# Last mixture of experts: second weights stationary in two parts, the activation evaluated twice, a feature-major output, gates spread by DMA, and one pipeline over all blocks

## The chip, the cores and the metric

The program runs on one core of a Trainium2 chip. The metric is device microseconds (us) of that core. The kernel before takes 2481.97 us, the median of 3 runs (2480.72 to 2484.28).

Engines are named as the profile names them: PE is TensorE's matmul and PEld its weight load, DVE is VectorE, ACT is ScalarE, POOL is GpSimd, SP is SyncE, which here only issues DMAs.

## What is computed

Four layers follow each other on x, of 4096 tokens by 128 features, each as `x = x + layernorm(layer(layernorm(x)))`. Only the last is touched: a mixture of 8 experts, each with a hidden width of 512, all of them evaluated for every token. Cut from the reference:

```python
logits = x @ router_W + router_b
w, idx = jax.lax.top_k(logits, K)            # K = 2
w = jax.nn.softmax(w, axis=-1)
gates = jnp.einsum('bske,bsk->bse', jax.nn.one_hot(idx, E), w)
xhat = (x - mu) * jax.lax.rsqrt(var + EPS)
h = xhat[:, :, None, :] * ln_g + ln_b
a = jax.nn.gelu(jnp.einsum('bseh,ehf->bsef', h, W1) + b1, approximate=False)
y = jnp.einsum('bsef,efh->bseh', a, W2) + b2
y = y + x[:, :, None, :]
out = jnp.einsum('bseh,bse->bsh', y, gates)
```

## The kernel before

Names of this layer's buffers begin with md_ in the profile. The 4096 tokens are 8 blocks (`NBLK`) of 512 tokens (`BLK`), a block is 4 tiles of 128 tokens (`BPT`), and the hidden width is 4 chunks of 128 (`FC`). One block of one expert is called an item here; there are 64.

**Setting up.** Row statistics of X, transposed and normalised tokens in two parts (`nh`, the rounded value, and `nl`, the rest), W1 in two parts (`wh`, `wl`), router logits, and the router, which leaves `gate` (token-major, 128 x 32 x 8) and `gsum`. W2 is loaded into `w2` as it is.

**The blocks.** PE, DVE, ACT and POOL each run a loop over the 8 blocks.

- PE, per item: 4 calls of `up`, each three matmuls of 512 columns (`matmul_split`, lines 64 to 66) into one bank of `ub`, in turn with 4 calls of `down`, each for one tile of 128 tokens: 4 matmuls at line 2332 with a slice of `a` stationary and W2 moving, in plain float32. The profile counts each such matmul as two records. `down` of an item begins when all four chunks are through ACT.
- ACT, per item: 4 Gelus of 128 x 512 from `ub` to `a` (line 2179).
- DVE, per block: the normalised tokens (2261), times `gsum` (2265), 32 additions of a bias times a gate (2270), then per item 4 additions of an output tile times its gate (2276), then the layer norm of the result (`FinishNorm.vector`, 1476 to 1489) with one power on POOL (1516) in its middle.
- SP stores each block when DVE is done with it (2154).

The output is token-major here: a gate is one number per partition, `gate[:, tile, e]`, and it enters DVE's instruction as that. At a block's end PE waits for all of its Gelus and additions:

```python
pe.wait_ge(gelu, (n + 1) * NE * FC)
pe.wait_ge(acc_done, n * NA + NA)
```

Of the kernel before, what the change touches and what calls it, by code (L numbers as in the profile page):

```python
# [2080 lines left out]
FC = FF // P  # L2081


def ffn_layer1(nc, dr, X, g, out):

    with Mem(nc, "d_") as m:
        wh = m.sb("wh", [P, NE, FF], F32R)
        wl = m.sb("wl", [P, NE, FF], F32R)
        w2 = m.sb("w2", [P, NE, FC, D])
        b1 = m.sb("b1", [P, NE, FC])  # L2090
        b2 = m.sb("b2", [P, NE, D])
# [23 lines left out]
        ub, db = bk[:, 0:FC, :], bk[:, FC:FC + 2, :]
        bp = bk[:, 2 * GRP - 1, :]

        w_in = m.sem("w_in")
# [14 lines left out]
        l_done = m.sem("l_done")  # L2133
        summed = m.sem("summed")
        ln = m.sem("ln")
        up_mm = m.sem("up_mm")
        gelu = m.sem("gelu")
        down_mm = m.sem("down_mm")
        acc_done = m.sem("acc_done")
        stored = m.sem("stored")  # L2140
        NA = BPT * (1 + 2 * NE)
        group = range(GRP)
        firsts = range(0, NBLK, GRP)
        with nc.Block() as block:
            @block.sync
            def _(sp):
                for dst, src in ((raw[:, :, :], "d_w1"), (lng[:, :], "d_lng"), (lnb[:, :], "d_lnb"),
                                 (rr[:, :], "d_wr"), (b1raw[:, :, :], "d_b1")):
                    sp.dma_start(dst, dr[src]).then_inc(w_in, 16)
                for dst, src in ((w2[:, :, :, :], "d_w2"), (b2[:, :, :], "d_b2"), (rbias[:, :], "d_rbias")):  # L2150
                    sp.dma_start(dst, dr[src]).then_inc(c_in, 16)
                with sp.Fori(0, NBLK) as n:
                    sp.wait_ge(F.step, n * F.N + F.N)
                    sp.dma_start(out.rearrange("(t p) d -> p t d", p=P)[:, bass.ds(n * BPT, BPT), :],
                                 X[:, bass.ds(n * BPT, BPT), :]).then_inc(stored, 16)
                sp.wait_ge(stored, 16 * NBLK)

            @block.scalar
            def _(act):
                act.wait_ge(w_in, 16 * 5)  # L2160
                nc.scalar.activation(wr[0][:, :], rr[:, :], ACT.Copy).then_inc(hi, 1)
                for e in range(NE):
                    nc.scalar.activation(wh[:, e, :], raw[:, e, :], ACT.Copy, scale=lng[:, e:e + 1]).then_inc(hi, 1)
                for n in firsts:
                    for i in group:
                        act.wait_ge(xt_mm, n + i + 1)
                        nc.scalar.activation(nh[:, (n + i) * BLK:(n + i + 1) * BLK], bk[:, 2 * i, :],
                                             ACT.Copy).then_inc(xh_done, 1)
                    for i in group:
                        act.wait_ge(l_mm, n + i + 1)  # L2170
                        nc.scalar.activation(lt[:, i, :], bk[0:32, 2 * i + 1, :], ACT.Copy).then_inc(l_copied, 1)
                router.scalar(nc, act)
                with act.Fori(0, NBLK) as n:
                    for e in range(NE):
                        for c in range(FC):
                            act.wait_ge(up_mm, (n * NE + e) * FC + c + 1)
                            if e >= 2 and c == 0:
                                act.wait_ge(down_mm, n * NE + e - 1)
                            nc.scalar.activation(a[:, e % 2, c, :], ub[:, c, :], ACT.Gelu,  # L2179
                                                 bias=b1[:, e, c:c + 1]).then_inc(gelu, 1)  # L2180

            @block.gpsimd
            def _(pool):
                stats_pool(nc, pool, S)
                with pool.Fori(0, NBLK) as n:  # L2185
                    F.pool(nc, pool, n, S)

            @block.vector
            def _(dve):
# [58 lines left out]
                dve.wait_ge(c_in, 16 * 3)  # L2248
                logits(0)
                low(GRP)  # L2250
                weights(range(NE // 2, NE))
# [5 lines left out]
                with dve.Fori(0, NBLK) as n:  # L2257
                    tiles = [bass.ds(n * BPT + s, 1) for s in range(BPT)]

                    for s in range(BPT):  # L2260
                        nc.vector.tensor_scalar(xi[:, s, :], X[:, tiles[s], :], S.mean[:, tiles[s], 0], S.r[:, tiles[s]],
                                                ALU.subtract, ALU.mult).then_inc(ln, 1)
                    for s in range(BPT):
                        dve.wait_ge(ln, n * BPT + s + 1)
                        nc.vector.tensor_scalar(acc[:, s, :], xi[:, s, :], gsum[:, tiles[s]], None,
                                                ALU.mult).then_inc(acc_done, 1)
                    for e in range(NE):
                        for s in range(BPT):
                            dve.wait_ge(acc_done, n * NA + e * BPT + s + 1)
                            nc.vector.scalar_tensor_tensor(acc[:, s, :], b2[:, e, :], gate[:, tiles[s], e], acc[:, s, :],  # L2270
                                                           ALU.mult, ALU.add).then_inc(acc_done, 1)
                    for e in range(NE):
                        dve.wait_ge(down_mm, n * NE + e + 1)
                        for s in range(BPT):
                            dve.wait_ge(acc_done, n * NA + (NE + e) * BPT + s + 1)
                            nc.vector.scalar_tensor_tensor(acc[:, s, :], db[:, e % 2, s * P:(s + 1) * P],  # L2276
                                                           gate[:, tiles[s], e], acc[:, s, :], ALU.mult,
                                                           ALU.add).then_inc(acc_done, 1)
                    dve.wait_ge(acc_done, n * NA + NA)
                    F.vector(nc, dve, n, acc, X, S)  # L2280

            @block.tensor
            def _(pe):
# [32 lines left out]
                pe.wait_ge(c_in, 16 * 3)  # L2316
                with pe.Fori(0, NBLK) as n:
                    cols = bass.ds(n * BLK, BLK)

                    def up(e, c):  # L2320
                        if e > 0:
                            pe.wait_ge(gelu, (n * NE + e - 1) * FC + c + 1)
                        cs = slice(c * P, (c + 1) * P)
                        matmul_split(nc, ub[:, c, :], wh[:, e, cs], wl[:, e, cs], nh[:, cols], nl[:, cols]).then_inc(up_mm, 1)

                    def down(e, s):
                        if s == 0:
                            pe.wait_ge(gelu, (n * NE + e + 1) * FC)
                            if e >= 2:
                                pe.wait_ge(acc_done, n * NA + (NE + e) * BPT)  # L2330
                        for c in range(FC):
                            last = nc.tensor.matmul(db[:, e % 2, s * P:(s + 1) * P], a[:, e % 2, c, s * P:(s + 1) * P],  # L2332
                                                    w2[:, e, c, :], start=(c == 0), stop=(c == FC - 1))
                        if s == BPT - 1:
                            last.then_inc(down_mm, 1)

                    for c in range(FC):
                        up(0, c)
                    for e in range(NE):
                        for s in range(BPT):  # L2340
                            if e + 1 < NE:
                                up(e + 1, s)
                            down(e, s)
# [16 lines left out]
def host_layout(a):  # L2360
# [54 lines left out]
    z["d_b2"] = np.broadcast_to(a["L1_ffn_b2"], (P, NE, D))  # L2415
# [27 lines left out]
```

## Time and profile before

| | us |
|---|---|
| median of 3 runs | 2481.97 |
| profiled execution, its own time | 2475.36 |
| its span, first to last instruction | 2473.6 |
| of it: last mixture, from its first load to the end | 1983.4 to 2473.6 |
| of it: first to last matmul of the blocks | 2026.3 to 2463.9 |

| engine | busy over the span | busy from 2030 to 2474 |
|---|---|---|
| PE | 2078.5 us (84%) | 417.55 us (94%) |
| DVE | 1605.4 us (65%) | 187.81 us (42%) |
| ACT | 999.2 us (40%) | 184.90 us (42%) |
| POOL | 655.3 us (26%) | 8.05 us (2%) |

Times in the rows are counted from the span's start. A row of the timeline is: start, duration, engine, line, operation, output <- input, count, and in brackets the idle time before it with what ended it. Neighbours of one kind are merged into a row with a count, so that duration over count is the pace at which they follow each other; the mean of one (in the groups by line) is longer than that, since neighbours overlap. PEclk is the granted clock of PE as a share of full speed.

### The profile page before, as it was taken

To read this page: it belongs to the slowest core of one execution; us is meant where nothing else is said; L and a number is where in the kernel's file an instruction comes from. 1 tells how busy PE (TensorE), PEld (TensorE's weight loads), DVE (VectorE), ACT (ScalarE), POOL (GpSimd) and SP (SyncE) were. 2 spreads that over 40 slices of the span, in tenths; PEclk is the share of its full clock that TensorE was granted. 3 is DMA by queue.
4 is the path that set the end of the run, shared out by engine and by line. 5 is a ranking of instruction groups with operands and counts; after the bars stand their busy time and mean duration, and the time that the engine had idled before them with its cause. 6 is when DMAs were issued, how large, how long until landed. Compare 5 with 4: busy or idle time off the path is not lost. (4 is left out here: it accounts for less than half of the span.)

```text
span 2473.6 us, 46736 instructions
## 1 busy us (share of the span) xinstructions
PE 2078.5 (84%) x16920; PEld 1650.4 (67%) x16920; DVE 1605.4 (65%) x4182; ACT 999.2 (40%) x1990; POOL 655.3 (26%) x409
## 2 busy tenths in 40 slices
PE   4888888884799988999768885889689869999998
PEld 3667767664456655666556774678477758888887
DVE  5776676774777737777377678677767775333344
ACT  2455455453155552555432222233223334444443
POOL 3545545543145551555400003000300010000000
PEclk9999999997599996999889998899899969999999
DMA  4111111111000000000000001000000020000000
GB/s 154 70 69 58 61 63 65 65 69 36 0 1 2 1 1 1 1 2 1 1 1 0 0 0 41 1 1 1 1 1 1 1 79 5 4 4 4 4 4 8
DMA packets 34795, 54.88 MB, mean 22 GB/s; under 512 B 7104, under 2 KB 16960, under 8 KB 33856
## 3 DMA queue, kind: packets, MB, share of 16 engines
q1 hardware_dynamic: 34624, 52.57, 5.8%
q8 instruction: 111, 1.82, 0.3%
q14 instruction: 60, 0.49, 0.1%
HBM read 16.90 MB, written 2.10 MB: 8 GB/s over the span
## 5 line engine op out<-in xcount | busy, mean ns | idle before, releaser
L1051 POOL TENSOR_TENSOR mb_psum<-mb_pt 128x1024 f32<-128x1024 f32 x112 | 267.1, 2387 | 313.5 <-ACT mb_pt L1031 312.8
L1031 ACT ACTIVATE mb_pt<-mb_stb 128x1024 f32<-128x1024 f32 x256 | 249.2, 1021 | 146.7 <-PE mb_stb L1132 146.2
L2332 PEld LDWEIGHTS md_bk<-md_w,md_a 128*128 128x128 f32 x2048 | 264.0, 192 | 26.2 <-ACT md_a L2179 3.9
L2179 ACT ACTIVATE md_a<-md_bk,md_b 128x512 f32<-128x512 f32 x256 | 175.5, 687 | 244.9 <-PE md_bk L66 244.5
L919 DVE TENSOR_REDUCE mb_mxp<-mb_p1b 128x1 f32<-128x512 f32 x352 | 231.1, 683 | 65.9 <-PE mb_p1b L1116 62.0
L2332 PE MATMUL md_bk<-md_w,md_a 128*128 128x128 f32 x2048 | 267.9, 276 | 2.7 <-DVE md_acc L2276 2.1
L2276 DVE SCALAR_TENSOR_TENSOR md_acc<-md_bk,md_gate,md_acc 128x128 f32<-128x128 f32 x256 | 71.9, 344 | 235.9 <-PE md_bk L2332 235.8
L351 DVE TENSOR_TENSOR ma_tr<-ma_pbank,ma_cs 128x512 f32<-128x512 f32 x256 | 161.6, 682 | 73.3 <-PE ma_pbank L66 69.2
L1955 ACT ACTIVATE mc_p<-mc_sb,mc_nb 128x512 f32<-128x512 f32 (+3 forms) x160 | 98.0, 621 | 186.9 <-DVE mc_nb L1843 186.9
L495 ACT ACTIVATE ma_e<-ma_sbank,ma_mx 128x80 f32<-128x80 f32 x512 | 120.3, 385 | 117.5 <-DVE ma_mx L358 117.5
L2033 PE MATMUL mc_pv<-mc_v,mc_pt 128*128 128x128 f32 x1088 | 149.8, 282 | 11.7 <-DVE mc_pt L1892 11.4
L1116 PE MATMUL mb_p1b<-mb_ks,mb_qs 96*128 96x512 f32 x352 | 152.6, 479 | 6.1 <-DVE mb_qs L912 2.8
L2033 PEld LDWEIGHTS mc_pv<-mc_v,mc_pt 128*128 128x128 f32 x1088 | 134.0, 192 | 23.0 <-DVE mc_pt L1892 18.7
L444 POOL TENSOR_TENSOR ma_qt<-ma_tr,ma_swp 128x512 f32<-128x512 f32 x64 | 88.1, 1378 | 224.3 <-DMA ma_swp<-ma_tr 217.8
L1132 PE MATMUL mb_stb<-mb_qs,mb_ks 98*128 98x512 f32 x512 | 144.7, 404 | 0.8 <-ACT mb_pt L1031 0.8
L1143 PE MATMUL mb_pvb<-mb_pt,mb_v 128*32 128x256 f32 x2048 | 137.0, 385 | 0.0
L64 PE MATMUL md_bk<-md_nh,md_wh 128*128 x256 | 122.9, 480 | 15.2 <-DVE md_acc L2276 12.5
L1516 POOL TENSOR_TENSOR md_frs<-md_fve,md_half 128x4 f32<-128x4 f32 x8 | 8.1, 1007 | 461.8 <-DVE md_fve L1481 461.8
L919 DVE TENSOR_REDUCE mb_mxp<-mb_misc 128x1 f32<-128x512 f32 x160 | 109.1, 682 | 22.0 <-PE mb_misc L1116 22.0
L64 PE MATMUL ma_pbank<-ma_xth,ma_wh 128*128 128x256 f32 x256 | 87.1, 340 | 38.5 <-DVE ma_tr L351 38.4
L1132 PEld LDWEIGHTS mb_stb<-mb_qs,mb_ks 98*128 98x128 f32 x512 | 94.6, 190 | 33.4 <-issue 12.4
L1833 DVE TENSOR_REDUCE mc_mp<-mc_sb 128x1 f32<-128x512 f32 (+3 forms) x160 | 96.6, 609 | 26.1 <-PE mc_sb L2012 13.8
(329 smaller groups left out, 4838.3 us busy)
## 6 DMA issues: line engine op xcount, KB each, us to landing
ma_swp<-ma_tr SPq DMA_DIRECT2D x256, 128.0 KB, 2.0
mg_X<-x SPq DMA_DIRECT2D x4, 512.0 KB, 10.4
ma_cs<-cs SPq DMA_DIRECT2D x1, 2048.0 KB, 9.4
mc_cs<-cs SPq DMA_DIRECT2D x1, 2048.0 KB, 8.1
md_raw<-d_w SPq DMA_DIRECT2D x1, 2048.0 KB, 7.3
md_w<-d_w SPq DMA_DIRECT2D x1, 2048.0 KB, 10.9
out<-mg_X SPq DMA_DIRECT2D x8, 256.0 KB, 2.3
ma_raw<-w_qkv SPq DMA_DIRECT2D x1, 1536.0 KB, 8.4
```

The lines of the kernel that those rows point to most:

```text
L64: nc.tensor.matmul(out, lhs_hi, rhs_hi, start=start, stop=False)
L351: nc.vector.tensor_tensor(tr[:, G % TRS, part, :, :], pbank[:, i % 2, :].rearrange("p (c t) -> p c t", c=2), cs[:, b // 2, part, None, :]. ...
L495: nc.scalar.activation(e[:, s, slot, :], sbank[:, 2 * j + k // 4, k % 4 * KEYS0:(k % 4 + 1) * KEYS0], ACT.Exp, bias=mx[:, s, slot:slot + 1 ...
L919: nc.vector.tensor_reduce(mxp[:, r // NCH, r % NCH:r % NCH + 1], pass_bank(r), AXX, ALU.max).then_inc(p1_max, 1)
L1031: nc.scalar.activation(pt[:, T % RING, :, :].rearrange("p (b h) q -> p b (h q)", b=2), stb[:, 2 * (i % 2):2 * (i % 2) + 2, :], ACT.Exp, sc ...
L1051: nc.gpsimd.tensor_tensor(psum[:, n % SUMS, :, :], pt[:, T % RING, :, :], pt[:, (T + 1) % RING, :, :], ALU.add).then_inc(summed, 1)
L1116: nc.tensor.matmul(pass_bank(r), qs[V % 3][0:QROWS, h, t * P:(t + 1) * P], ks[0:QROWS, c * BLK:(c + 1) * BLK], start=True, stop=True).then ...
L1132: last = nc.tensor.matmul(stb[:, 2 * (i % 2) + hp, :], ks[:, i * P:(i + 1) * P], qs[U % 3][:, 2 * hp:2 * hp + 2, :].rearrange("p h q -> p ...
L1143: last = nc.tensor.matmul(pvb[h * DK:(h + 1) * DK, 0:UQ], v1[:, i, :], pt[:, T % RING, h, :], start=(i == 0), stop=(i == KT - 1), skip_gro ...
L2033: last = nc.tensor.matmul(pv[:, 0:D], pt[:, k % 2, a * P:(a + 1) * P], v[:, c * BPT + a, :], start=(c == 0 and a == 0), stop=(c == chunks[ ...
L2179: nc.scalar.activation(a[:, e % 2, c, :], ub[:, c, :], ACT.Gelu, bias=b1[:, e, c:c + 1]).then_inc(gelu, 1)
L2332: last = nc.tensor.matmul(db[:, e % 2, s * P:(s + 1) * P], a[:, e % 2, c, s * P:(s + 1) * P], w2[:, e, c, :], start=(c == 0), stop=(c == F ...
```

## The change

- **W2 in two parts.** `w2` is replaced by `w2h`, the rounded value (8 copies on ACT, 2216), and `w2l`, the rest (8 subtractions on POOL). The load goes into `late`, whose room later holds the spread gates `gb` (4 rows of 128 x 512), the accumulators `accT` (2) and `tmp` (2).
- **Feature-major output.** `down` works by chunks: three matmuls of 512 columns with a chunk of W2 stationary and the hidden values moving, accumulated over the 4 chunks into a bank of `db` that holds 128 features by 512 tokens.
- **The hidden values in two parts.** ACT evaluates each chunk twice, in full to `a` (2230) and rounded to `ah` (2236), for chunks 0 to 2; chunk 3's rounded value is a copy on DVE. DVE subtracts: `al = a - ah`, 4 per item.
- **Gates.** They now run along the free axis and must be the same on all partitions. Per block PE transposes `gate` to 8 x 512 (2456), ACT copies it to `gT` on partitions 0 to 7 (2223), and SP spreads one row per item over 128 partitions: 64 DMAs of 256 KB whose source is a single partition (2193). DVE then does one `(db + b2) * gb` per item, and POOL adds it to the accumulator.
- **Back to tokens.** Per block PE transposes the accumulator back (2489), and DVE finishes the block in 13 parts (`finish`), two places per item, during later items. The power on POOL and the stores on SP are placed among other items' work too.
- **No loops, no waits at a block's end.** Each engine's 64 items are written out. The DMA for item j is issued when item j-4 has been scaled, and DVE waits for item j's row before it scales item j.

```diff
 @block.sync
-with sp.Fori(0, NBLK) as n:
-    sp.wait_ge(F.step, n * F.N + F.N)
-    sp.dma_start(out..., X[:, bass.ds(n * BPT, BPT), :]).then_inc(stored, 16)
+for j in range(ITEMS):
+    n, e = divmod(j, NE)
+    if e == 0:
+        sp.wait_ge(gT_done, n + 1)
+    if j >= GB:
+        sp.wait_ge(scaled, j - GB + 1)
+    sp.dma_start(gb[:, j % GB, :], gT[e:e + 1, n % 2, None, :].to_broadcast([1, P, BLK])).then_inc(gb_in[j % GB], 16)
+    if e == STORE_AT[1] and n >= STORE_AT[0]:
+        store(n - STORE_AT[0])
 @block.scalar
-nc.scalar.activation(a[:, e % 2, c, :], ub[:, c, :], ACT.Gelu, bias=b1[:, e, c:c + 1]).then_inc(gelu, 1)
+turn_gates(0)
+for j in range(ITEMS):
+    for c in range(FC):
+        hidden(j, c)
+        if c < HIA:
+            high(j, c)
+    if e == GATE_AT and n + 1 < NBLK:
+        turn_gates(n + 1)
 @block.gpsimd
+for e in range(NE):
+    pool.wait_ge(w2_hi, e + 1)
+    nc.gpsimd.tensor_tensor(w2l[:, e, :, :], w2raw[:, e, :, :], w2h[:, e, :, :].bitcast(F32), ALU.subtract)
+for j in range(ITEMS):
+    if e > 0:
+        pool.wait_ge(scaled, j + 1)
+        nc.gpsimd.tensor_tensor(accT[:, n % 2, :], accT[:, n % 2, :], tmp[:, e % 2, :], ALU.add).then_inc(added, 1)
 @block.vector
+def scale(j):
+    dve.wait_ge(down_mm, (j + 1) * FC)
+    dve.wait_ge(gb_in[j % GB], 16 * (j // GB + 1))
+    nc.vector.scalar_tensor_tensor(dst, db[:, j % 2, :], b2[:, e:e + 1], gb[:, j % GB, :], ALU.add, ALU.mult)
+for j in range(ITEMS):
+    low(j, 0)
+    low(j, 1)
+    finish_at(2 * j)
+    high(j, 3)
+    low(j, 2)
+    if j > 0:
+        scale(j - 1)
+    low(j, 3)
+    finish_at(2 * j + 1)
 @block.tensor
-def down(e, s):
-    for c in range(FC):
-        last = nc.tensor.matmul(db[:, e % 2, s * P:(s + 1) * P], a[:, e % 2, c, s * P:(s + 1) * P],
-                                w2[:, e, c, :], start=(c == 0), stop=(c == FC - 1))
-pe.wait_ge(gelu, (n + 1) * NE * FC)
-pe.wait_ge(acc_done, n * NA + NA)
+def down(j, c):
+    if j >= 2:
+        pe.wait_ge(scaled, j - 1)
+    pe.wait_ge(lo_done, j * FC + c + 1)
+    matmul_split(nc, db[:, j % 2, :], w2h[:, e, c, :], w2l[:, e, c, :], ah[:, c, :], al[:, c, :],
+                 start=(c == 0), stop=(c == FC - 1)).then_inc(down_mm, 1)
```

On PE, one piece of an item. In the kernel before, in the loop over the blocks:

```order
L64 MATMUL md_bk<-md_nh,md_wh 128x512
L65 MATMUL md_bk<-md_nh,md_wl 128x512
L66 MATMUL md_bk<-md_nl,md_wh 128x512
L2328 ISA
L2330 REGISTER_ALU
L2332 MATMUL md_bk<-md_w,md_a 128x128 x4
```

The same place in the changed kernel, at the item in which the accumulator of the block before is turned back (`md_late`):

```order
L64 MATMUL md_bk<-md_nh,md_wh 128x512
L65 MATMUL md_bk<-md_nh,md_wl 128x512
L66 MATMUL md_bk<-md_nl,md_wh 128x512
L2489 MATMUL md_bk<-mg_ident,md_late 128x128 x4
L64 MATMUL md_bk<-md_ah,md_w2h 128x512
L65 MATMUL md_bk<-md_ah,md_w2l 128x512
L66 MATMUL md_bk<-md_al,md_w2h 128x512
```

Three float32r matmuls of 512 columns stand where four float32 matmuls of 128 columns stood; the transposes come once per block.

On SP, the queue of the stores, `+` and `-` as the change makes them:

```order
-L2154 DMA out<-mg_X 128x4x128
-L2152 REGISTER_ALU
-L2152 COMPARE_AND_BRANCH
-L2144 UNCONDITIONAL_BRANCH
...
+L2179 DMA md_late<-d_w 128x4096
+L2193 DMA md_late<-md_raw 128x1x512 x23
+L2184 DMA out<-mg_X 128x4x128
+L2193 DMA md_late<-md_raw 128x1x512 x8
+L2184 DMA out<-mg_X 128x4x128
```

A loop with nothing but stores became a queue in which 23 spreads of a gate row (`md_late<-md_raw` is `gb` from `gT`) stand ahead of the first store and 8 ahead of each later one, until the last two blocks.

On ACT, the end of setting up and the first item:

```order
+L2216 ACTIVATE md_w2h<-md_late 128x512 x8
 L1544 ACTIVATE md_r_ex<-md_r_df 128x32
```

The 8 roundings of W2 now stand ahead of the router's exponential.

## Rows read from the trace of the kernel before

**Rows 1.** Busy time and clock over the blocks (engines, PEclk, DMA share, GB/s).

```profile
2030.00:2474.00 444.00, 417.55 (x2804) 377.41 (x2804) 187.81 (x769) 184.90 (x264) 8.05 (x8) 0.97 0.02 5
```

**Rows 2.** Groups by line, 2030 to 2474: count, busy us, mean ns, idle before.

```profile
L2332 PE MATMUL md_bk<-md_w,md_a 128*128 128x128 f32 x2048 | 267.9, 276 | 2.7 <-DVE md_acc L2276 2.1 <-ACT md_a L2179 0.4
...
L2179 ACT ACTIVATE md_a<-md_bk,md_b 128x512 f32<-128x512 f32 x256 | 175.5, 687 | 244.9 <-PE md_bk L66 244.5
...
L2276 DVE SCALAR_TENSOR_TENSOR md_acc<-md_bk,md_gate,md_acc 128x128 f32<-128x128 f32 x256 | 71.9, 344 | 235.9 <-PE md_bk L2332 235.8
```

**Rows 3.** Timeline, PE inside a block: one `up` and one `down`.

```profile
2201.71 0.48 PE L64 MATMUL md_bk<-md_nh,md_wh 128*128 x1
...
2202.26 0.39 PE L66 MATMUL md_bk<-md_nl,md_wh 128*128 x1
...
2202.49 1.05 PE L2332 MATMUL md_bk<-md_w,md_a 128*128 128x128 f32 x8
...
2203.29 0.48 PE L64 MATMUL md_bk<-md_nh,md_wh 128*128 x1
```

**Rows 4.** Timeline, PE from one block into the next.

```profile
2197.38 0.63 PE L65 MATMUL md_bk<-md_nh,md_wl 128*128 x1
...
2197.81 0.63 PE L66 MATMUL md_bk<-md_nl,md_wh 128*128 x1
```

**Rows 5.** Timeline of neighbours on ACT and DVE; one DVE line.

```profile
2030.45 3.00 ACT L2179 ACTIVATE md_a<-md_bk,md_b 128x512 f32<-128x512 f32 x5
...
2020.37 2.48 DVE L2204 TENSOR_TENSOR md_nl<-md_bk,md_nh 128x512 fp32r<-128x512 f32 x4 [0.62 <-ACT md_nh L2167]
...
2022.77 2.73 DVE L2225 SCALAR_TENSOR_TENSOR md_wl<-md_raw,md_lng,md_wh 128x512 fp32r<-128x512 f32 x4
...
L1632 DVE TENSOR_SCALAR mb_rq<-mb_rq,mb_g x1: 415/415/415, 613.0 to 613.0; 128x384 f32<-128x384 f32 x1
```

**Rows 6.** Timeline, DVE finishing one tile by rows, in the layer before.

```profile
1979.50 0.35 DVE L1508 TENSOR_SCALAR mc_acc<-mc_acc,mc_fmv,mc_frs 128x128 f32<-128x128 f32 x1 [1.12 <-POOL mc_frs L1516]
...
1980.20 0.34 DVE L1508 TENSOR_SCALAR mc_acc<-mc_acc,mc_fmv,mc_frs 128x128 f32<-128x128 f32 x1
```

**Rows 7.** Timeline, POOL and DVE on two SBUF inputs together, and POOL alone.

```profile
1526.37 1.30 POOL L1913 TENSOR_TENSOR mc_rp<-mc_tr 128x512 f32<-128x512 f32 x1 [0.68 <-DVE mc_tr L1803]
...
1526.39 1.83 DVE L1809 TENSOR_TENSOR mc_kql<-mc_rp,mc_kqh 128x512 fp32r<-128x512 f32 x1
...
L446 POOL TENSOR_TENSOR ma_kt<-ma_tr,ma_swp x64: 1262/1275/2331, 48.2 to 556.3; 128x512 f32<-128x512 f32 x64
```

**Rows 8.** DMA: issues (KB each, us to landing), and a stretch of loads.

```profile
ma_swp<-ma_tr SPq DMA_DIRECT2D x256, 128.0 KB, 2.0
...
out<-mg_X SPq DMA_DIRECT2D x8, 256.0 KB, 2.3
...
1988.00:1996.00 8.00, 1.61 (x7) 1.17 (x7) 7.79 (x54) 3.62 (x7) 8.00 (x4) 0.50 1.00 410
```

**Rows 9.** Timeline, start of the blocks on PE, ACT and DVE.

```profile
2019.05 1.97 PE L2291 MATMUL md_bk<-mg_ident,md_xn 128*128 128x128 f32 x16
...
2026.31 0.49 PE L64 MATMUL md_bk<-md_nh,md_wh 128*128 x1 [0.89 <-DVE md_lg L2212]
...
2022.18 2.69 ACT L2171 ACTIVATE md_lt<-md_bk 32x512 f32<-32x512 f32 x4 [0.38 <-PE md_bk L66]
...
2029.15 1.28 ACT L2179 ACT_TABLE_LOAD   x1
...
2036.24 0.42 DVE L2255 TENSOR_REDUCE md_gsum<-md_gate 128x32 f32<-128x256 f32 x1
```

**Rows 10.** Timeline, tail: DVE, POOL and SP after the last item.

```profile
2459.01 4.85 PE L2332 MATMUL md_bk<-md_w,md_a 128*128 128x128 f32 x40
...
2466.71 1.01 POOL L1516 TENSOR_TENSOR md_frs<-md_fve,md_half 128x4 f32<-128x4 f32 x1 [52.59 <-DVE md_fve L1481]
...
2469.89 0.38 SPq L2154 DMA_DIRECT2D out<-mg_X  x1
```

More of the change, by code:

```diff
@@ L2081 @@
 FC = FF // P
+GB = 4
+GATE_AT = 3
+STORE_AT = (2, 6)
+POWER_AT = (1, 4)
+APPLY = (10, 12)
+FINISH_AT = 2 * (NE + 2)
 def ffn_layer1(nc, dr, X, g, out):
@@ L2105, in ffn_layer1 @@
         gsum = m.sb("gsum", [P, TILES])
+        ah = m.sb("ah", [P, FC, BLK], F32R)
+        al = m.sb("al", [P, FC, BLK], F32R)
         xn = m.sb("xn", [P, GRP, BPT, D])
@@ L2135, in ffn_layer1 @@
         ln = m.sem("ln")
+        w2_in = m.sem("w2_in")
+        w2_hi = m.sem("w2_hi")
+        w2_lo = m.sem("w2_lo")
         up_mm = m.sem("up_mm")
         gelu = m.sem("gelu")
+        hi_act = m.sem("hi_act")
+        hi_dve = m.sem("hi_dve")
+        lo_done = m.sem("lo_done")
         down_mm = m.sem("down_mm")
-        acc_done = m.sem("acc_done")
+        scaled = m.sem("scaled")
+        added = m.sem("added")
+        gT_mm = m.sem("gT_mm")
+        gT_done = m.sem("gT_done")
+        gb_in = [m.sem(f"gb_in{k}") for k in range(GB)]
+        turned = m.sem("turned")
+        row_sum = m.sem("row_sum")
         stored = m.sem("stored")
-        NA = BPT * (1 + 2 * NE)
+        ITEMS = NBLK * NE
+        HIA = FC - 1
         group = range(GRP)
@@ L2247, in _ @@
                 dve.wait_ge(inv_step, 2)
-                dve.wait_ge(c_in, 16 * 3)
+                dve.wait_ge(c_in, 16 * 2)
                 logits(0)
@@ L2256, in _ @@
                 dve.wait_ge(summed, 1)
[L2257 to L2280, printed above, removed]
@@ new lines, in finish @@
+                def finish(n, part):
+                    s = part // 2
+                    if part < 2 * BPT:
+                        if part % 2 == 0:
+                            residual(n, s)
+                            total(n, s)
+                        else:
+                            dve.wait_ge(row_sum, n * BPT + s + 1)
+                            F.row_stats(nc, dve, n, s, acc)
+                    elif part in APPLY:
+                        for k in range(2):
+                            s = 2 * APPLY.index(part) + k
+                            F.apply(nc, dve, n, s, acc, X, n * BPT + s)
@@ new lines, in _, with finish_at @@
+                PARTS = APPLY[-1] + 1
+                def finish_at(t):
+                    n, part = divmod(t - FINISH_AT, 2 * NE)
+                    if 0 <= n < NBLK and part < PARTS:
+                        finish(n, part)
+                for j in range(ITEMS):
[8 more added lines that the diff above has]
+                    finish_at(2 * j + 1)
@@ L2282, in _ @@
+                scale(ITEMS - 1)
+                for t in range(2 * ITEMS, FINISH_AT + 2 * NE * (NBLK - 1) + PARTS):
+                    finish_at(t)
             @block.tensor
@@ new lines, in _, with turn_gates, up @@
+                pe.wait_ge(c_in, 16 * 2)
+                def turn_gates(n):
+                    pe.wait_ge(summed, 1)
+                    if n > 0:
+                        pe.wait_ge(gT_done, n)
+                    for s in range(BPT):
+                        last = nc.tensor.transpose(gtb[:, s * P:(s + 1) * P], gate[:, n * BPT + s, :], ident[:, :])
+                    last.then_inc(gT_mm, 1)
+                def up(j, c):
+                    n, e = divmod(j, NE)
+                    cols = slice(n * BLK, (n + 1) * BLK)
+                    cs = slice(c * P, (c + 1) * P)
+                    if j >= 1:
+                        pe.wait_ge(gelu, (j - 1) * FC + c + 1)
+                        if c < HIA:
+                            pe.wait_ge(hi_act, (j - 1) * HIA + c + 1)
+                    matmul_split(nc, ub[:, c, :], wh[:, e, cs], wl[:, e, cs], nh[:, cols], nl[:, cols]).then_inc(up_mm, 1)
@@ new lines, in turn_back @@
+                def turn_back(n):
+                    pe.wait_ge(added, (n + 1) * (NE - 1))
+                    if n > 0:
+                        pe.wait_ge(row_sum, n * BPT)
+                    for s in range(BPT):
+                        last = nc.tensor.transpose(fb[:, s * P:(s + 1) * P], accT[:, n % 2, s * P:(s + 1) * P], ident[:, :])
+                    last.then_inc(turned, 1)
+                for c in range(FC):
+                    up(0, c)
+                turn_gates(0)
+                for j in range(ITEMS):
+                    n, e = divmod(j, NE)
+                    for c in range(FC):
+                        if j + 1 < ITEMS:
+                            up(j + 1, c)
+                        if c == 2 and e == GATE_AT and n + 1 < NBLK:
+                            turn_gates(n + 1)
+                        if c == 2 and e == 1 and n > 0:
+                            turn_back(n - 1)
+                        down(j, c)
@@ L2348, in rope_tables @@
+                turn_back(NBLK - 1)
 def rope_tables(n, d, scale):
```

132 lines of the change are left out of this document (92 added, 40 removed).

## Prediction

> **What bounds the kernel now.** I read the busy times first: over the blocks of the last mixture PE is busy 417.55 of 444 us, at 0.97 of full clock, while DVE and ACT have less than 190 us of work each and the DMA engines almost none [rows 1]. Then the groups by line: ACT's Gelus sat idle 244.5 us for PE and DVE's additions 235.8 us, whereas the matmuls of `down` waited 2.7 us in all [rows 2]. So PE sets the pace, and in the timeline one reads off what it is made of. Inside a block an `up` and a `down` follow each other every 2203.29 - 2201.71 = 1.58 us [rows 3], four times per item: 6.32 us, and 64 items are 404.5 us. The matmuls run from 2026.31 to 2463.86 [rows 9, 10], which is 437.5 us. The other 33 us lie at the start and at the block ends, where PE stands still and then runs at half clock: a matmul of 512 columns follows the last after 0.43 us there [rows 4] and after 0.23 us inside a block [rows 3].
>
> **What the change takes from PE.** `up` stays: three matmuls at 0.23, 0.695 us. `down` of one tile took 1.58 - 0.695 = 0.885 us; it becomes the same triple as `up`, 0.695 us. An item then costs PE 8 x 0.695 = 5.56 us in place of 6.32, and 64 cost 356 us. Transposes are added, 8 per block at 1.97/16 = 0.12 us [rows 9], with their breaks some 8 us in all. The stops at the block ends go, if nothing else is late.
>
> **ACT.** Seven evaluations per item instead of four. Their mean is 0.687 us [rows 2] but neighbours follow at 3.00/5 = 0.60 [rows 5], so 4.2 us per item, 4.8 if each took its full mean. Both are under 5.56. One copy of gates per block adds 0.6 us. The table load of 1.28 us, once per block before, now comes once.
>
> **DVE.** Per item: four subtractions at 2.48/4 = 0.62 (the form of the row is the same but reads one input from PSUM), one rounding copy, at 128 x 512 scaled from 0.415 us for 384 columns to about 0.5, one scaling by the spread gates at 2.73/4 = 0.68 [rows 5]. That is 3.7 us. The finish of a block costs per tile four short instructions of at most 0.345 us [rows 2] with a break of 0.1 between dependents, 1.6 us, and 0.70 us for the last two [rows 6]; four tiles 9.2 us, 1.15 per item. Sum 4.8 us, under 5.56.
>
> **POOL.** One addition of 128 x 512 in 7 of 8 items, 1.27 us alone [rows 7], hidden by far. But it does not leave DVE alone. In the layer before, a DVE subtraction of two SBUF inputs that began 0.02 us behind a POOL addition took 1.83 us and ended 0.55 us behind the other's end [rows 7]; alone such a one takes about 0.68. So DVE stood still for the whole of POOL's 1.27. At worst this adds 1.1 us to an item: 4.8 + 1.1 = 5.9 us. The addition comes right behind DVE's scaling, with one subtraction in front of it and the finish parts behind, so I take less than half.
> The Trainium skill has this as a rule ("SBUF — State Buffer", section "Who interferes with whom": a DVE instruction with two SBUF inputs contends with a GpSimd instruction that reads SBUF, and the second fully blocks). The row agrees with it.
>
> **The gates' DMAs.** Per item SP spreads one row of 2 KB, on one partition, over 128: 256 KB. They are issued four items ahead, about 16 us before they are needed at 5.56 per item, so latency is no question; what matters is how often one can be served. No row shows a source on a single partition, so I bound it.
> - From below: 128 KB from 64 partitions to 64 others lands after 2.0 us and 256 KB from 128 partitions to memory after 2.3 [rows 8]. At that price the DMAs are hidden with 3 us to spare per item.
> - From above: in the busiest 8 us of loads 16 DMA engines moved 410 GB/s at a busy share of 1.00 [rows 8], 25.6 GB/s each. Each then had 8 partitions of its own. If the limit is the way into those partitions rather than the engine, sixteen engines reading one partition share one such way: 262144 B / 25.6 GB/s = 10.2 us per item, almost twice what PE needs.
> The loads came from memory, which may have slowed them a little; I take 9.5 us for a copy inside SBUF, and keep 10.2. Between 2.3 and 9.5 I take the upper end, with some doubt: the steady, even share of the sixteen in the loads looks like sixteen separate ways, and none of these rows has more than one engine at one partition.
> The Trainium skill puts it as a rule ("SBUF — State Buffer", section "Door 1: The DMA port swizzle": partitions map to 16 ports, and a transfer reaches only the ports of its partitions, 27.2 GB/s each). One partition is one port, and by its figure a row would take 9.6 us, 64 of them 617 us; by the landing times above it would cost nothing. Nothing in this trace tests it for a read.
>
> **Setting up and the tail.** The router's end stays at 2036.66 [rows 9]. The 8 roundings of W2 (0.6 each) stand between ACT's last copy at 2024.87 and the router's exponential, done by 2029.9, while DVE still looks for indices until 2033.3; POOL's 8 subtractions end 8 x 1.27 behind 2025.6, at 2035.8. So neither is late. But ACT now waits for the gates before its first Gelu: transposes 0.5, copy 0.6, breaks 0.2, first spread issued at 2038.0, table load, first Gelu at 2039.4, where it was 2030.45 [rows 5]. That costs about 9 us of start. Tail, behind the last matmul or the last gate row: scaling 0.85, addition 1.4, transposes 0.7, four tiles at 1.6, power 1.4, four at 0.7, store and landing 2.7, in all 16 us; before it was 9.7 (2463.86 to the end).
>
> **The sum.** If one partition limits the DMAs: 2038.0 + 64 x 9.5 + 1.7 (fixed part of a landing) = 2647.7, tail 16, span 2663.5. The profiled execution took 1.8 more than its span and the median lies 6.6 above that: 2663.5 + 8.4 = **2672 us**. At 10.2 it is 2717. That PE idles 4 us per item then and may lose clock is covered: even at 0.43 us per matmul in part of an item it has 9.5.
>
> **Rivals.**
> 1. *The DMAs are hidden and PE bounds* (faster, the other side). From 2040.8: 63 x 2.78 + 64 x 2.78 = 353, transposes 8, filling and small stalls 10, PE ends at 2412; tail 16, span 2428: **2436 us** (2425 to 2450). For it speak the landing times of 2.0 and 2.3; against it, that none has a single source partition. It decides at a price per DMA of about 5.7 us: below, this is the result.
> 2. *The DMAs are hidden, and DVE and POOL take turns.* 6.0 us per item with breaks, 64 x 6.0 = 384, from 2040.8 and with the tail: 2441, or **2450 to 2465 us** with the transposes' stalls. For it speaks the 1.83; against it, that DVE has unshared work (scaling, statistics) to lay beside the addition.
> 3. *The row is served at half of an engine's rate*, since one partition is an eighth of what an engine served: 19 us per item, past 3200 us. I see no row for it.
>
> **How the numbers follow.** One-partition limit at 9 to 10.2 us per row: 0.56. Rival 1: 0.31. Rival 2: 0.09. Rival 3 or another slow case: 0.02. A DMA price between 6 and 7 that ends near the old time: 0.02. The forecast's own range is 2640 to 2720. Over all cases 8 in 10 need both sides: 2426 to 2720. About 0.2% is what a measurement of this kernel can tell from no change. Faster 0.40, same 0.01, slower 0.59.
>
> **What would show it.** Right: the spread DMAs land 25 to 40 us behind their issue (four are queued), the DMA queue moves about 27 GB/s through the whole stage, DVE's scaling waits for the DMA, PE is busy about 60% of an item, and POOL, ACT and DVE idle. Rival 1: landing near 2.5 us, PE over 95% busy at full clock, an item every 5.6 us. Rival 2: DVE over 95% with subtractions of 1.2 us and more in each item. The PE step is wrong if a triple of `down` is not 0.70 us; ACT's is if its pace is nearer 0.69 than 0.60. The forecast falls as a whole if one partition can feed more than 46 GB/s (256 KB in 5.7 us).

## The result, and the profile after

The changed kernel takes 2639.16 us (median of 4 runs, 2636.08 to 2640.48); the kernel before took 2483.12 beside it. The ratio is 1.063 (95% interval 1.061 to 1.065): slower by 156 us, all of it in the last mixture. The layers ahead are the same code, but they end up to 11 us earlier or later from one execution to the next. So this text measures the *stage*: from the MEMSET of line 714, with which DVE enters the last mixture, to the end of the span. Each stage is that of one profiled execution; differences of 1 or 2 us between stages are not read. Before it was 2473.6 - 1983.49 = 490.1 us, after it is 2636.5 - 1991.20 = 645.3.

The page of the kernel after, part 1, and of part 2 the granted clock, the DMA engines' busy tenths and what they moved, in 40 slices of 66 us. The last nine slices are the blocks of the last mixture:

```profile
PE 2098.4 (80%) x15704; PEld 1600.2 (61%) x15704; DVE 1751.6 (66%) x4054; ACT 1120.0 (42%) x2191; POOL 758.8 (29%) x473
...
PEclk8999999996899969998799879998996798888887
DMA  4111111110000000000000100000001788888886
GB/s 144 67 63 65 65 65 59 67 38 33 1 1 1 1 1 1 1 1 1 0 0 0 38 1 1 1 2 1 1 1 66 25 32 32 34 34 32 34 34 35
```

The DMA engines, all but idle before at this place (share 0.02, 5 GB/s in [rows 1]), are now 80 to 90% busy in seven of the last nine slices and yet move only 32 to 34 GB/s there. A stretch of loads moved 410 at share 1.00 [rows 8]. Then 50 us inside the blocks as a window (columns as in [rows 1]), and below it two short stretches, which are used further down:

```profile
2150.00:2200.00 50.00, 40.25 (x148) 29.70 (x149) 31.29 (x61) 27.62 (x43) 12.01 (x8) 0.90 0.88 33
...
2145.00:2155.00 10.00, 7.65 (x26) 5.52 (x26) 5.04 (x10) 3.40 (x5) 1.67 (x1) 0.84 0.90 27
2155.50:2158.50 3.00, 2.94 (x15) 1.96 (x13) 0.00 (x0) 1.42 (x3) 0.00 (x0) 1.00 0.85 49
```

PE is busy 80% of the 50 us, at a granted clock of 0.90 in the mean, where it was 94% busy at 0.97 over the blocks before. No engine is full. The issues of DMAs (KB each, median us to landing):

```profile
md_late<-md_raw SPq DMA_DIRECT2D x64, 256.0 KB, 29.9
...
out<-mg_X SPq DMA_DIRECT2D x8, 256.0 KB, 19.7
```

The spread rows land 29.9 us behind their issue. The stores, same size and same queue, needed 2.3 us before [rows 8] and now 19.7: they wait their turn behind the spreads. Who waits, over 2040 to 2637 (total us, times, longest):

```profile
DVE md_late L2364 <- issue: 196.3, 43, 6.6
...
PE md_bk L64 <- DVE md_al L2344: 126.2, 50, 3.9
ACT md_raw L2230 <- DVE md_al L2344: 105.7, 44, 3.8
...
DVE md_late L2364 <- DMA md_late<-md_raw: 25.7, 5, 5.5
```

Line 2364 is the scaling by the spread gates. DVE stands in front of it 43 times, and the view gives "issue", which means that it saw nothing that released it. Only in 5 cases does it name the DMA. In 8 more (22.3 us) it names PE's L66, and the matmuls of PE show that this is not what held DVE (one of the 8):

```profile
2150.96 0.40 PE L66 MATMUL md_bk<-md_al,md_w2h 128*128 128x512 f32 x1
...
2157.35 0.39 PE L66 MATMUL md_bk<-md_al,md_w2h 128*128 128x512 f32 x1
...
2158.74 0.75 DVE L2364 SCALAR_TENSOR_TENSOR md_late<-md_bk,md_b,md_late 128x512 f32<-128x512 f32 x1 [4.59 <-PE md_bk L66]
```

The scaling at 2158.74 needs the four chunks of its item. The last of them is the first row, done at 2151.36; the second row belongs already to the next item. In all 8 the item's last matmul began 4.4 us or more ahead of its scaling. What holds DVE there is read from the rhythm, in the timeline of DVE, and of SP's DMA issues at the same time (the second fence):

```profile
2300.86 0.75 DVE L2364 SCALAR_TENSOR_TENSOR md_late<-md_bk,md_b,md_late 128x512 f32<-128x512 f32 x1 [2.23 <-PE md_bk L66]
...
2310.88 0.75 DVE L2364 SCALAR_TENSOR_TENSOR md_late<-md_bk,md_b,md_late 128x512 f32<-128x512 f32 x1 [4.80 <-issue]
...
2320.68 0.75 DVE L2364 SCALAR_TENSOR_TENSOR md_late<-md_bk,md_b,md_late 128x512 f32<-128x512 f32 x1 [5.15 <-issue]
2321.34 2.37 DVE L2344 TENSOR_TENSOR md_al<-md_raw,md_ah 128x512 fp32r<-128x512 f32 x2
```

```profile
2289.43 17.45 SPq L2193 DMA_DIRECT2D md_late<-md_raw  x2
2306.93 9.73 SPq L2184 DMA_DIRECT2D out<-mg_X  x1
2316.71 34.68 SPq L2193 DMA_DIRECT2D md_late<-md_raw  x5
```

Scaling comes every 9.8 us where PE needs 5.6 per item, and SP is itself held 9.7 us inside a single issue, as if the queue took a new transfer only when an old one had gone. 262144 B / 9.8 us = 26.75 GB/s. Behind the scaling the last subtractions (L2344) are late, and behind those PE and ACT. The chain that ended last has 6% of the span on this DMA, the most of any line.

The triple of `down` in the timeline of PE (forecast 0.70 us for three):

```profile
2300.72 0.39 PE L64 MATMUL md_bk<-md_ah,md_w2h 128*128 128x512 f32 x1
2300.95 0.39 PE L65 MATMUL md_bk<-md_ah,md_w2l 128*128 128x512 f32 x1
2301.18 0.39 PE L66 MATMUL md_bk<-md_al,md_w2h 128*128 128x512 f32 x1
2301.41 0.40 PE L64 MATMUL md_bk<-md_nh,md_wh 128*128 128x512 f32 x1
```

2301.41 - 2300.72 = 0.69 us. At the start of the stage's blocks, POOL, ACT and DVE, beside [rows 9]:

```profile
2033.17 9.89 POOL L2253 TENSOR_TENSOR md_w2l<-md_late,md_w2h 128x512 fp32r<-128x512 f32 x8 [27.61 <-ACT md_w2h L2216]
...
2026.97 0.49 DVE L2299 TENSOR_TENSOR md_lg<-md_lg,md_rbias 128x32 f32<-128x32 f32 x4
...
2033.53 4.70 DVE L2299 TENSOR_TENSOR md_lg<-md_lg,md_rbias 128x32 f32<-128x32 f32 x4
2040.57 1.35 DVE L1571 TENSOR_TENSOR md_r_df<-md_r_top 128x32 f32<-128x32 f32 x1
2049.28 0.42 DVE L2335 TENSOR_REDUCE md_gsum<-md_gate 128x32 f32<-128x256 f32 x1
```

Four additions of 32 columns take 0.49 us without POOL and 4.70 beside POOL's subtractions for W2. That is 1.18 us for each, near the 9.89 / 8 = 1.24 us at which POOL's subtractions follow each other: about one small addition per subtraction. L1571 was 0.23 before. The router ends 2049.70 - 1991.20 = 58.5 us behind the stage's start, where it was 2036.66 - 1983.49 = 53.2 before [rows 9].

### The profile page after: what moved, and what is told of

It reads as the page before. It is cut to its first block and busy times, and to the rows that moved or that the text cites. A ratio compares the mean times of both kernels' runs of the same rounds, so it can differ in the third digit from the quotient of the medians.

```text
span 2636.5 us, 44065 instructions
## 1 busy us (share of the span) xinstructions
PE 2098.4 (80%) x15704; PEld 1600.2 (61%) x15704; DVE 1751.6 (66%) x4054; ACT 1120.0 (42%) x2191; POOL 758.8 (29%) x473
## 2 busy tenths in 40 slices
DMA packets 44037, 71.44 MB, mean 27 GB/s; under 512 B 8256, under 2 KB 18112, under 8 KB 43072
## 5 line engine op out<-in xcount | busy, mean ns | idle before, releaser
L2230 ACT ACTIVATE md_raw<-md_bk,md_b 128x512 f32<-128x512 f32 x256 | 175.5, 686 | 182.0 <-DVE md_al L2344 105.7
L2261 POOL TENSOR_TENSOR md_late<-md_late 128x512 f32<-128x512 f32 x56 | 92.9, 1659 | 475.7 <-DVE md_late L2364 475.7
L64 PE MATMUL md_bk<-md_ah,md_w2h 128*128 128x512 f32 x256 | 121.4, 474 | 127.6 <-DVE md_al L2344 126.2
L2344 DVE TENSOR_TENSOR md_al<-md_raw,md_ah 128x512 fp32r<-128x512 f32 x256 | 206.8, 838 | 6.9 <-ACT md_ah L2236 6.9
L2364 DVE SCALAR_TENSOR_TENSOR md_late<-md_bk,md_b,md_late 128x512 f32<-128x512 f32 x64 | 48.0, 750 | 244.3 <-issue 196.3
L64 PEld LDWEIGHTS md_bk<-md_ah,md_w2h 128*128 128x128 f32 x256 | 55.7, 218 | 170.6 <-issue 160.9
L2236 ACT ACTIVATE md_ah<-md_bk,md_b 128x512 fp32r<-128x512 f32 x192 | 131.8, 686 | 34.2 <-PE md_bk L66 27.4
L1516 POOL TENSOR_TENSOR mc_frs<-mc_fve,mc_half 128x4 f32<-128x4 f32 x8 | 8.1, 1011 | 374.8 <-DVE mc_fve L1500 374.8
## 6 DMA issues: line engine op xcount, KB each, us to landing
md_late<-md_raw SPq DMA_DIRECT2D x64, 256.0 KB, 29.9
out<-mg_X SPq DMA_DIRECT2D x8, 256.0 KB, 19.7
```

The costliest lines, as they stand in the source:

```text
L64: nc.tensor.matmul(out, lhs_hi, rhs_hi, start=start, stop=False)
L2230: nc.scalar.activation(a[:, c, :], ub[:, c, :], ACT.Gelu, bias=b1[:, e, c:c + 1]).then_inc(gelu, 1)
L2236: nc.scalar.activation(ah[:, c, :], ub[:, c, :], ACT.Gelu, bias=b1[:, j % NE, c:c + 1]).then_inc(hi_act, 1)
L2344: nc.vector.tensor_tensor(al[:, c, :], a[:, c, :], ah[:, c, :].bitcast(F32), ALU.subtract).then_inc(lo_done, 1)
```

## The experiments

**Another source for the same row.** Main theory: a transfer whose source is one partition runs at the pace of the way into the small group of partitions that holds it. Rivals: the engines or the queue are slow on this shape whatever the source is, or the amount written is the limit. Four kernels leave the destination and the bytes alone, or change only those.

*e1_16copies.* POOL repeats the block's gates 16 times (0.6 to 1.1 us per block), the transposes are 128 wide, so that all 128 partitions hold rows, and one DMA reads its row on 16 of them:

```diff
-sp.dma_start(gb[:, j % GB, :], gT[e:e + 1, n % 2, None, :].to_broadcast([1, P, BLK]))
+sp.dma_start(gb[:, j % GB, :], gT[e::NE, n % 2, None, :].to_broadcast([P // NE, NE, BLK]))
```

> Each gate row is repeated on 16 partitions (e, e+8, ... e+120) by a POOL copy of the gates ahead of the transposes, and one DMA per item still moves 256 KB, now from 16 partitions with 8 targets each. Nothing else changes, and the output is complete. Theory (one partition is reached by one way of about 27 GB/s, which all 16 DMA engines share): with 16 partitions the DMA lands in about 3 us, DVE no longer waits for it, PE bounds at 5.6 to 5.9 us per item, and the time is about 2440 us (2425 to 2465). Rival A (a source that is repeated is slow in itself, or SP needs 9 us to issue such a DMA): still about 2640. Rival B (DVE and POOL taking turns is what really paces the item at near 8.9 us): still above 2600 with the DMA landing early.

*e2_alt64* keeps these 128 copies but reads one partition again, in turn e and e + 64; *e3_alt32* is the same with 32:

```diff
+r = e + 64 * (j % 2)
+sp.dma_start(gb[:, j % GB, :], gT[r:r + 1, n % 2, None, :].to_broadcast([1, P, BLK]))
```

> Gates repeated as in the run with 16 copies, but each DMA reads a single partition again: partition e for even items and e+64 for odd ones. Theory, with the way shared by a group of partitions (0 to 3 one, 4 to 7 another, as the 49 GB/s at the change from expert 3 to 4 suggests) and another group beyond 64: neighbours in the queue read two groups, 2 x 26.75 GB/s = 4.9 us per item, so PE or DVE bounds and the time is 2440 to 2480. Rival (the limit is the DMA as such, one single-partition source at a time): 2640.

> As the run that alternates e and e+64, but with e and e+32. If the way is shared by a group of partitions that holds p and p+32 (the Trainium skill's port map says so), nothing is gained: 2640 (2630 to 2650), rows still 9.8 us apart. Rival (each partition, or each block of 4 neighbours, has a way of its own): the same as with e+64, 2440 to 2480.

*e4_half* is the changed kernel with half of each row spread:

```diff
-sp.dma_start(gb[:, j % GB, :], gT[e:e + 1, n % 2, None, :].to_broadcast([1, P, BLK]))
+sp.dma_start(gb[:, j % GB, 0:256], gT[e:e + 1, n % 2, None, 0:256].to_broadcast([1, P, 256]))
```

> The changed kernel, but each DMA spreads only the first 256 of 512 columns, 128 KB from one partition; the other half of the tokens is scaled by what stands in the buffer, so half of the gates are left out. Theory (a price per byte of 1/26.75 us per KB and little fixed): 4.9 us per item, hidden, 2440 to 2470. Rival (a fixed price per DMA or per row of its 128 targets, about 9.8 us): 2640.

Measured:

| | time, us | ratio to before (95%) | stage, us | landing, us |
|---|---|---|---|---|
| changed kernel | 2639.16 | 1.063 (1.061 to 1.065) | 645.3 | 29.9 |
| e1_16copies | 2440.95 | 0.984 (0.983 to 0.986) | 447.4 | 3.0 |
| e2_alt64 | 2436.02 | 0.982 (0.980 to 0.984) | 448.6 | 13.1 |
| e3_alt32 | 2632.67 | 1.062 (1.060 to 1.064) | 646.3 | 29.9 |
| e4_half | 2436.37 | 0.983 (0.982 to 0.985) | 446.7 | 6.5 |

The windows of one stretch, of e1, of e2 and of e3 (columns as above):

```profile
2150.00:2200.00 50.00, 49.88 (x218) 39.59 (x217) 43.24 (x81) 39.51 (x63) 15.54 (x10) 1.00 0.22 49
```

```profile
2150.00:2200.00 50.00, 49.88 (x218) 39.62 (x217) 43.28 (x79) 39.53 (x63) 15.31 (x11) 1.00 0.83 51
```

```profile
2150.00:2200.00 50.00, 40.13 (x151) 30.34 (x150) 30.94 (x56) 30.53 (x47) 12.52 (x8) 0.90 0.87 33
```

With 16 source partitions the DMA share falls to 0.22 and PE is never idle: the same 256 KB are written in as many packets (44037 in both executions), so the destination and the amount are not the limit. e2 and e3 differ in one number, 64 or 32. With 64 the queue moves 51 GB/s from single partitions and PE is full, with 32 nothing changes. So it is neither "one partition" as such nor the queue. Partitions 32 apart share one way of 26.75 GB/s, and those 64 apart do not. Several transfers are in progress together (a row lands 29.9 us behind its issue, and rows are 9.8 us apart), and two of them gain only if their sources lie on different ways. e4 says the same of the amount: with half the bytes per DMA the limit is gone, which a fixed price per DMA would not give.
This is the map that the Trainium skill gives ("SBUF — State Buffer", section "Door 1: The DMA port swizzle": adding 32 to a partition stays on its port, adding 64 changes to the other one, and 4 neighbouring partitions share one). It states 27.2 GB/s per port, beside 26.75 here.

**Where the shorter intervals come from.** In the changed kernel scaling follows scaling after 9.8 us, but at two places in each block after less. The first of one block: 2158.74, 2163.89, 2173.19. The mean is 8.87 us per row. The rows lie on partitions 0 to 7, and the map above puts 0 to 3 on one way and 4 to 7 on another. Then two rows overlap when the next expert's row lies across that border, from 3 to 4 and from 7 to 0. These three scalings are those of experts 2, 3 and 4, so the short interval stands in front of expert 3's and not of expert 4's. Some three rows are in progress together, and in the short stretch shown above, 2155.5 to 2158.5, the queue moves 49 GB/s instead of 27, before row 3 has been used. That row 4 is moved beside the others then is read from this rate; no view shows single transfers. Two kernels leave everything alone but which row is read:

```diff
-... gT[e:e + 1, n % 2, None, :] ...
+... gT[0:1, n % 2, None, :] ...                                # e9_row_0_only
+... gT[4 * (j % 2):4 * (j % 2) + 1, n % 2, None, :] ...        # e10_rows_0_and_4
```

> The changed kernel, but all 64 spreads read the same row, that of partition 0; everything else is untouched. Left out are the gates of the seven other experts, so the time is that of the transfers and not of another amount of work. Theory (a transfer runs at the pace of the group of partitions that holds its source, and the changed kernel's mean of 8.87 us per row comes from 9.8 us inside a group and two overlaps per block, where the row moves from partition 3 to 4 and from 7 to 0): there are no overlaps left, each of the 64 rows takes 9.8 us, the last scaling begins 64 x 9.8 = 627 us behind the first issue in place of 569, the stage is 645.3 + 58 = 703 us, and the time some 2697 us. In every stretch of 10 us of the stage the queue moves 27 to 28 GB/s. Rival (the shorter intervals are an effect of the block's end, of the copy of gates or of the stores): they stay where they are and the time stays within 5 us of 2639.

> The changed kernel, but the 64 spreads read the rows of partitions 0 and 4 in turn; everything else is untouched. Left out are the gates of the six other experts. Theory: neighbours in the queue always lie in different groups of four partitions, so that two are served at once at 26.75 GB/s each; a row then costs 4.9 us, less than PE's 5.6 per item, the transfers are hidden as with partitions 64 apart, the stage is about 447 to 449 us, the time some 2436 to 2440 us, and landing takes about 13 us. Rival (only the other half of the partitions, 64 away, is another way, and what shortens the interval from expert 3 to 4 is something else): nothing is gained, and the time is 2639 or more, up to 2697 us.

e9 took 2700.76 us, ratio 1.091 (1.087 to 1.094), stage 707.9, landing 33.6. e10 took 2444.38, ratio 0.985 (0.984 to 0.987), stage 452.1, landing 14.8. The scaling line of e9 (durations in ns, then first and last start), then a window of e9 and the same of e10:

```profile
L2364 DVE SCALAR_TENSOR_TENSOR md_late<-md_bk,md_b,md_late x64: 744/751/752, 2058.1 to 2677.9; 128x512 f32<-128x512 f32 x64
```

```profile
2200.00:2210.00 10.00, 7.41 (x26) 5.33 (x25) 5.67 (x9) 4.76 (x7) 1.67 (x1) 0.84 0.90 27
```

```profile
2200.00:2210.00 10.00, 10.00 (x47) 8.13 (x46) 7.75 (x15) 7.90 (x13) 0.64 (x2) 1.00 0.81 53
```

(2677.9 - 2058.1) / 63 = 9.84 us per row when no two sources differ, and 53 to 54 GB/s in four windows of 10 us when neighbours alternate between partitions 0 and 4. The same four windows of e9 show 27, 27, 27 and 29 GB/s, the last one more than the 27 to 28 that were expected. The first kernel fixes the pace of one way, the second shows that the way belongs to a group of four neighbours at most; that neighbours inside the group share it is shown by the changed kernel, whose rows of experts 0, 1 and 2 come 9.8 us apart. Both stages are 3 to 5 us over what was expected of them. In e9 the short intervals in front of expert 3 are gone in all eight blocks. One short interval stays, 5.66 us in front of expert 6 in each of the last five blocks, where a store stands behind that row in the queue. The interval after it is long, 13.6 to 14.6 us in four of the five, so that the two together take 19.3 to 20.3 us, about two full rows: for this place the rival was right, but the pace does not gain by it. The first store of e9 costs one interval of 12.3 us. That the stores take part of the way would fit all this; it was not followed up.

**At which size it decides.** *e7_three_quarters* spreads 384 of 512 columns (the diff of e4 with 384):

> The changed kernel, each DMA spreading 384 of 512 columns from its one partition; a quarter of the gates is left out. Theory (price by bytes, 9.8 us per full row, with two overlaps per block, so 8.9 per item on average): 0.75 x 8.9 = 6.7 us per item against the 5.76 at which PE runs in the run with 16 copies, stage 447 + 64 x 0.92 = 506 us, time about 2498 (2485 to 2510). Rival (a threshold in something else, such as a full buffer): either 2440 or 2640.

It took 2492.59 us, ratio 1.004 (1.003 to 1.005), stage 501.3 us, landing 22.9. Its rows take 7.4 us inside a group of partitions (9.8 x 0.75 = 7.35), with the same overlaps. At half the size (4.9 us by proportion) PE bounds, at three quarters the transfers do, and the stage is 501.3 - 446.7 = 54.6 us longer than with half rows, which is more than the 490.1 - 446.7 = 43.4 us that the change gains when the transfers are hidden. The forecast's break-even, 5.7 us per DMA, lies between the two sizes.

**DVE and POOL.** *e8_small_add* is e1 with POOL's addition cut to 16 columns:

```diff
-nc.gpsimd.tensor_tensor(accT[:, n % 2, :], accT[:, n % 2, :], tmp[:, e % 2, :],
+nc.gpsimd.tensor_tensor(accT[:, n % 2, 0:16], accT[:, n % 2, 0:16], tmp[:, e % 2, 0:16],
```

> As the run with 16 copies, but POOL adds only 16 of 512 columns, so the sum over the experts is left out for the rest. Theory (POOL's additions block DVE's subtractions of two SBUF inputs, but PE bounds): the subtractions' mean falls from 0.84 to 0.69 us, 0.6 us of DVE per item, and the stage stays within 2 us of 447.4. If DVE or POOL were part of the bound, the stage would fall by 10 us or more.

It took 2436.89 us (2 runs), ratio 0.982 (0.980 to 0.983), stage 445.2 us against 447.4 of e1. The subtractions and the addition by line over 2060 to 2500, first of e1, then of e8 (mean ns behind the busy time):

```profile
L2358 DVE TENSOR_TENSOR md_al<-md_raw,md_ah 128x512 fp32r<-128x512 f32 x253 | 204.8, 835 | 30.7 <-ACT md_ah L2238 30.6
...
L2275 POOL TENSOR_TENSOR md_late<-md_late 128x512 f32<-128x512 f32 x56 | 93.3, 1666 | 262.3 <-DVE md_late L2378 262.3
```

```profile
L2358 DVE TENSOR_TENSOR md_al<-md_raw,md_ah 128x512 fp32r<-128x512 f32 x251 | 169.2, 690 | 48.4 <-ACT md_ah L2238 47.7
...
L2275 POOL TENSOR_TENSOR md_late<-md_late 128x16 f32<-128x16 f32 x56 | 33.1, 591 | 316.4 <-DVE md_late L2378 316.4
```

POOL's addition costs DVE 204.8 - 169.2 = 36 us in this window, and the stage 2.2 us at most. DVE has the room: the contention is real and hidden.

**The start.** *e5_w2_early* is e1 with ACT's roundings of W2 moved ahead, so that POOL's subtractions lie in front of the router's last part; *e6_both_early* adds that ACT's and PE's work on the first gates comes behind item 0's Gelus:

```diff
@@ e5: ACT, behind the first group's copies of nh
+                    if n == 0:
+                        act.wait_ge(w2_in, 16)
+                        for e in range(NE):
+                            nc.scalar.activation(w2h[:, e, :, :], w2raw[:, e, :, :], ACT.Copy).then_inc(w2_hi, 1)
@@ e6: ACT, and PE behind up(1, 0)
-                turn_gates(0)
                 for j in range(ITEMS):
...
+                    if j == 0:
+                        turn_gates(0)
```

> As the run with 16 copies, with the 8 roundings of W2 on ACT moved ahead: from behind ACT's last copy of the logits to behind its first four copies of the tokens, while ACT and DVE wait for PE's bias matmuls. POOL's 8 subtractions then run there too. Theory (POOL's subtractions block DVE in the router: one of its additions took 4.70 us for four where it took 0.48, another 1.35 where it took 0.23): the last mixture, from its first memset to the end of the span, shrinks by 5 us from 447.4 to about 442; in the time 2441 to about 2436. Rival (the router is later for another reason, ACT's exponential): no change. A further 1 us may be lost if the first rounding delays the copies of the second group of tokens.

> As the run with W2 rounded early, and the first block's gates are turned behind the first item's Gelus on ACT and behind its second up on PE, instead of ahead of all of them. Theory (ACT's wait for the gates held the first Gelu back by about 9 us, of which DVE, busy with the router, would hold back all but 4 to 5): stage 437 to 438 us, time about 2431. Rival (the first items wait for DVE in any case): 442, no gain.

e5 took 2438.42 us, ratio 0.983 (0.981 to 0.984), stage 443.0; e6 took 2428.13, ratio 0.979 (0.977 to 0.980), stage 437.2. In e5, POOL and DVE's additions, and then e6's first Gelu:

```profile
2010.95 9.86 POOL L2256 TENSOR_TENSOR md_w2l<-md_late,md_w2h 128x512 fp32r<-128x512 f32 x8 [3.01 <-ACT md_w2h L2216]
...
2035.97 0.49 DVE L2314 TENSOR_TENSOR md_lg<-md_lg,md_rbias 128x32 f32<-128x32 f32 x4
...
2046.39 0.42 DVE L2350 TENSOR_REDUCE md_gsum<-md_gate 128x32 f32<-128x256 f32 x1
```

```profile
2033.77 0.69 ACT L2233 ACTIVATE md_raw<-md_bk,md_b 128x512 f32<-128x512 f32 x1
```

The additions are back at 0.49 us, and the router ends 2046.81 - 1993.57 = 53.2 us behind the stage's start, as before the change. (The stage of e1 was 447.4.) That the medians of e1 and e5 lie only 2.5 us apart, with the stages 4.4 apart, is the layers ahead, which end 1.2 us later in e5, and the distance of the profiled execution from the median. In e6 the first Gelu stands 47.0 us behind the stage's start instead of 57.0 in e5; 5.8 us of these 10 reach the end: PE now does the first `up` of item 1 and then stands 5.12 us in front of the transposes, for the gates. e6 leaves nothing out. It is 2.1% faster than the kernel before (2.0 to 2.3), and 211 us faster than the changed one.

## Why the prediction was right

The forecast was 2672 us, the time 2639: the sign and the cause held, and 33 us lie between. The time lies inside the range over all cases (2426 to 2720), and 1 us below the range that the forecast gave for its own case (2640 to 2720).

- **The gates' DMAs as the bound: right.** Of the two bounds, 2.3 us from landing times and 10.2 from the loads' rate per engine, the upper one was the right neighbour. Its signs came for the most part: landing at 29.9 us (said 25 to 40), DVE's scaling late. The queue moves 27 GB/s only inside a group and 32 to 34 through the stage, where 27 was said for all of it, and PE is busy 80% of the window instead of 60, with shorter intervals and at a clock of 0.90. The reason of the step was stated with doubt, and e1, e2 and e3 have shown it. The landing times of [rows 8] could not show this limit: 64 or 128 source partitions use many ways at once.
- **The price: 9.5 us, 9.8 in fact, and 8.87 in the mean.** What failed is the term 64 x 9.5. It took the transfers one behind the other, but the queue has several in progress, and at two borders per block two ways work together. From the first issue at 2051.48 to the last scaling at 2620.68, less 1.7, it is 8.87 x 64; that is 40.5 us less than forecast. e9 with no border costs 9.84 per row and 2701 us, e10 with only borders is free of the limit.
- **The start: wrong by 13.5 us.** First issue forecast at 2038.0, seen at 2051.48. Of this 7.7 us are the layers ahead (1991.20 against 1983.49) and no error of the step. 5.3 us are the sentence "neither is late" on W2's roundings and POOL's subtractions. It asked only when they end, not whom they hold up on the way: POOL's subtractions read SBUF while DVE adds two SBUF operands. [Rows 7] had shown just this stall, and I used it for the items and not for the router. e5 moved them and got 5.0 back (58.2 in e1 to 53.2). The Trainium skill's rule ("SBUF — State Buffer", section "Who interferes with whom"), quoted in the prediction for the items, covers this place too: a DVE instruction with two SBUF inputs contends with a GpSimd instruction that reads SBUF. The 4.70 us beside POOL and the 0.49 us without it agree.
- **So the sum**: 40.5 too much for the rows, 13.5 too little for the start, tail 15.8 against 16: 27 us of span too high (the forecast's own 2647.7 + 16 is 2663.7, not 2663.5, which changes nothing). The other 6 are the distance from the profiled run to the median, 6.6 before and 0.9 now.
- **PE's triple, ACT and the tail: right.** 0.69 us, ACT's neighbours at 0.57 (Gelus that start at 2053.87 and 2054.44), 15.8 us behind the last scaling. PE's clock fell to 0.84 in 2145 to 2155, and no cost of it shows, as said: DVE still stood 4.59 us in front of the scaling at 2158.74, whose matmuls had long been done.
- **DVE and POOL: size off, place right.** An addition took 1.66 us instead of 1.27, and the subtractions 0.84 in the mean. DVE is busy 43.2 of 50 us in e1 and bounds nothing. Rival 2 is out, by e8.
- **Rival 1 was the right value of the other side**: 2436 us if the DMAs are hidden; e1, e2 and e4 gave 2441, 2436 and 2436. So PE's sum holds in the state which the change reaches only with another source of the rows: the stage was put at 2428 - 1983.5 = 444.5 us, and was 447.4, 448.6 and 446.7. That two of the times agree to 0.4 us is in part luck: the layers ahead ended between 1 us earlier and 9 us later than in the kernel before, and 8.4 us were added to the span where 0.7 to 7.0 were right. The chance of 0.31 for it stood for one thing that the trace before could not show.

## What to carry to other kernels

A transfer that reads one partition, as each spread of a row over the others does, is bound by the way into that partition: it costs its bytes over some 27 GB/s, which the landing times of transfers from many partitions do not show. Ask how many such ways the source reaches and how often the transfer comes; the cure is in the layout of the source (here about 1 us of copying on POOL for each block). More buffers or an earlier issue would not change the 9.8 us per row, by this account; no run here tried them. When work is put on POOL "in the shadow", list the DVE instructions with two SBUF operands that run at that time.

## What the runs showed of the hardware that was not expected

- Consecutive transfers of one queue overlap, if their sources lie on different ways: 53 GB/s with partitions 0 and 4 in turn, 27 with 0 alone, 33 with e and e + 32, 51 with e and e + 64.
- A queue with its transfers waiting holds the issuing engine: SP stood 8.3 us in the median inside the issue of a spread (up to 9.8) in the changed kernel, and 0.53 us in e1. The stores behind it landed after 19.7 us instead of 2.3, and 3.4 in e1. Here SP had nothing else to do.
- The view of waits puts such a stall down to "issue" (196.3 us) and names the DMA for 25.7 us only; for 22.3 us it names matmuls of the next item. The even distance of 9.8 us was the better sign.
